# A routed layer on 28 tiles of 128 tokens in place of 32 batches of 112

## What is computed

```python
def _L3_ffn_ref(tokens, router_w, router_b, expert_weights):      # tokens 32 x 112 x 256
    logits = jnp.einsum('bsh,eh->bse', tokens, router_w) + router_b        # 8 experts
    probs = jax.nn.softmax(logits, axis=-1)
    top_p, top_i = jax.lax.top_k(probs, 2)
    w = top_p / (jnp.sum(top_p, axis=-1, keepdims=True) + EPS)
    y_all = jnp.einsum('nh,ehd->ned', x, expert_weights)                  # every token, every expert
    out = jnp.einsum('nk,nkh->nh', wf, y_k)                               # the two chosen, weighted
    ...
x = x + jnp.tanh(g_xattn[3]) * _L3_xattn_ref(_layernorm(x), ctx_1024, ctx_1024, mask, gamma, beta)
x = x + jnp.tanh(g_ffn[3]) * _L3_ffn_ref(_layernorm(x), router_w, router_b, expert_weights)
```

## Time and profile before

| | |
|---|---|
| median of 3 runs | 3184.21 us (3181.15 to 3189.6) |
| the profiled execution | 3165.71 us |
| its span, first to last instruction | 3163.5 us |
| PE busy | 3026.6 us, 96% |
| DVE busy | 2022.8 us, 64% |
| `masked_attention`, in the span | about 2789 to 2910 us |
| `routed_layer`, in the span | 2911 to 3163.5 us |

### The profile page before, as it was taken

One profiled execution on the slowest core, in us unless ns is written; L12 is line 12 of the kernel. 1 busy time (PEld: TensorE's weight loads), 2 busy tenths in 40 slices (PEclk: granted clock), 3 DMA queues, 4 the chain that ended last, 5 costly groups with the idle time before them and its releaser, 6 DMA issues. The chain is left out here.

```text
span 3163.5 us, 61263 instructions
## 1 busy us (share of the span) xinstructions
PE 3026.6 (96%) x23544; PEld 2306.6 (73%) x23544; DVE 2022.8 (64%) x4390; ACT 1456.5 (46%) x2845; POOL 626.3 (20%) x903
## 2 busy tenths in 40 slices
PE   8988999989899999999999999799999999899999
PEld 7875655667799999999999998566666666566443
DVE  4664111157577887778788876566666666588654
ACT  3431111135455555555555555466666666455000
POOL 3575000053000230122022000211112111045000
PEclk8998999999899999999999999899999999899999
DMA  9643233177200000000000000100000000255000
GB/s 275 185 145 115 80 120 120 54 212 247 83 2 1 2 2 1 2 1 2 1 2 2 1 1 2 36 16 21 20 18 21 16 21 11 76 171 168 15 15 18
DMA packets 75073, 181.80 MB, mean 57 GB/s; under 512 B 12102, under 2 KB 18739, under 8 KB 74453
## 3 DMA queue, kind: packets, MB, share of 16 engines
q1 hardware_dynamic: 58260, 137.83, 13.7%
q10 hardware_dynamic: 10192, 25.30, 2.6%
q0 software_dynamic: 6336, 14.76, 1.6%
HBM read 150.25 MB, written 27.79 MB: 56 GB/s over the span
## 5 line engine op out<-in xcount | busy, mean ns | idle before, releaser
L2786 ACT ACTIVATE probs<-probs,neg_top 112x375 f32<-112x375 f32 x512 | 281.8, 599 | 16.2 <-DVE neg_top L2709 15.0
L2709 DVE CUSTOM_DVE_ANT_0 probs<-ps,add 112x375 f32<-112x375 f32 x512 | 250.2, 546 | 58.8 <-PE ps L2860 55.1
L2266 DVE TENSOR_REDUCE top<-ps 112x16 f32<-112x1792 f32 x96 | 194.3, 2024 | 58.4 <-PE ps L2504 56.8
L3324 PE MATMUL ps<-we,xn_t 128*112 128x512 f32 x512 | 230.0, 613 | 0.9 <-PEq L813 0.9
L1646 DVE TENSOR_TENSOR hidden<-gated,ps 128x512 f32<-128x512 f32 x64 | 44.0, 688 | 284.6 <-PE ps L1689 284.6
L2716 DVE COPY probs_t<-ps 125x336 f32<-125x336 f32 x256 | 128.8, 503 | 151.4 <-PE ps L2887 151.4
L2887 PE MATMUL ps<-ident,probs 112*125 112x112 f32 x1536 | 222.5, 281 | 2.8 <-DVE probs_t L2716 2.8
L2887 PEld LDWEIGHTS ps<-ident,probs 112*125 112x125 f32 x1536 | 189.7, 188 | 30.7 <-issue 20.2
L2282 DVE TENSOR_TENSOR probs<-probs,inv_sum 112x1792 f32<-112x1792 f32 x96 | 197.2, 2054 | 3.3
L2278 DVE TENSOR_REDUCE row_sum<-probs 112x16 f32<-112x1792 f32 x96 | 193.9, 2020 | 4.3 <-ACT probs L2390 4.3
L2270 DVE TENSOR_TENSOR probs<-ps,top 112x1792 f32<-112x1792 f32 x96 | 194.3, 2024 | 3.3
(11 more groups left out here) (453 smaller groups left out, 6368.1 us busy)
## 6 DMA issues: line engine op xcount, KB each, us to landing
ctx_t<-in_ctx_T_dram SPq DMA_DIRECT2D x96, 375.0 KB, 4.4
ctx_sb<-in_ctx_dram ACTq DMA_DIRECT2D x64, 384.0 KB, 4.7
ctx_sb<-in_ctx_dram SPq DMA_DIRECT2D x32, 384.0 KB, 4.7
ctx_sb<-in_ctx_T_dram SPq DMA_DIRECT2D x32, 375.0 KB, 3.0
queue<-zeros SPq DMA_DIRECT2D x32, 256.0 KB, 5.2
rows<-queue SPq DMA_DIRECT2D x16, 512.0 KB, 4.8
outputs<-out SPq DMA_DIRECT2D x16, 512.0 KB, 2.9
mask_in<-in_mask_BxSxS_fk_dram SPq DMA_DIRECT2D x16, 328.1 KB, 5.8
```

The lines of the kernel that those rows point to most:

```text
L2266: dve.tensor_reduce(top[:, :, :], scores, AX.X, ALU.max).then_inc(s["top_done"], 1)
L2709: dve.tensor_tensor_reduce(out=probs[:, u, h, :], in0=k.ps[0:S, SCORE + h, 0:L], in1=add[:, j % 2, :], scale=1.0, scalar=BIG, op0=ALU.add, ...
L2786: act.activation(probs[:, u, h, :], probs[:, u, h, :], ACT.Exp, bias=neg_top[:, u, h:h + 1], scale=-1.0).then_inc(s["probs_done"], 1)
L3324: mm = pe.matmul(k.ps[0:S, Y + at % YB, :], xn_t[:, j + u, c, :], r.we[:, c, e:e + TWO, :].rearrange("p e d -> p (e d)"), start=c == 0, st ...
```

## The change

The routed layer takes the tokens in 28 tiles of 128 in place of 32 batches of 112.

- `x_sb` stays as it is for norms and transposes. A second tensor `x_tiles[128, 28, 256]` takes the same values as tiles. SP copies batch j into it after `residual_done` of that batch, by transfers from SBUF to SBUF (`load_routed_tiles`): a batch falls into one or two tiles, so each group of 8 batches takes 14 transfers of 112, 16+96, 32+80, 48+64, 64+48, 80+32, 96+16 and 112 rows of 1 KB, 56 in all. In SP's list those of batch j - 9 stand at the end of step j, those of the last nine batches behind the loop.
- The transposed tokens `xn_t` are stored as one row of 3584 tokens per chunk, so that a slice of 128 can straddle two batches. Transposes and copies out of PSUM stay at 112 tokens, 32 of each.
- `experts` runs over 14 pairs of tiles with 128 stationary columns; `routed_logits` runs 28 times instead of 32, each waiting for the batches under its tile; the add writes `x_tiles` and once a tile waits for `tiles_loaded` of its group of 7 tiles. `route_batches` and the other steps between the pairs stand behind the same pair numbers as before.
- The groups of `route_group` are 6, 8 and 14 tiles (before 8, 8 and 16 batches), and the logits of each tile have a place of their own in the PSUM bank.
- The output is stored from `x_tiles`, two tiles at a time, 14 stores.

```diff
@@ -67,7 +67,7 @@
-            sp.wait_ge(k.stored, 16 * (B // 2))
+            sp.wait_ge(k.stored, 16 * (TILES_R // 2))
...
-ROUTES = (0, NB, BODY, B)
+TILES_R = B * S // P
+TILES_G = NB * S // P
+ROUTES = (0, 6, 2 * TILES_G, TILES_R)
...
 def routed_copy(k, r, act, j):
 
     act.wait_ge(r.transposed, j + 1)
-    act.activation(r.xn_t[:, j, :, :], k.ps[:, R_XT + j % 2, 0:DC * S].rearrange("p (a t) -> p a t", a=DC), ACT.Copy).then_inc(r.xt_copied, 1)
-
-
-def routed_logits(k, r, pe, j, at):
-
-    pe.wait_ge(r.xt_copied, j + 1)
-    if j == 0:
+    act.activation(r.xn_t[:, :, j * S:(j + 1) * S], k.ps[:, R_XT + j % 2, 0:DC * S].rearrange("p (a t) -> p a t", a=DC), ACT.Copy).then_inc(r.xt_copied, 1)
+
+
+def routed_logits(k, r, pe, t):
+
+    pe.wait_ge(r.xt_copied, ((t + 1) * P + S - 1) // S)
+    if t == 0:
         pe.wait_ge(r.router_loaded, 32)
     for c in range(DC):
-        mm = pe.matmul(k.ps[0:S, R_LOGITS, at:at + E3], r.xn_t[:, j, c, :], r.rw_t[:, c, :], start=c == 0, stop=c == DC - 1)
+        mm = pe.matmul(k.ps[:, R_LOGITS, t * E3:(t + 1) * E3], r.xn_t[:, c, t * P:(t + 1) * P], r.rw_t[:, c, :], start=c == 0, stop=c == DC - 1)
     mm.then_inc(r.logits_done, 1)
+
+
+def routed_pieces(j):
+
+    first = j * S
+    out = []
+    while first < (j + 1) * S:
+        t, p = divmod(first, P)
+        count = min(P - p, (j + 1) * S - first)
+        out.append((first - j * S, count, t, p))
+        first += count
+    return out
...
+def load_routed_tiles(k, r, sp, j):
+
+    for s0, count, t, p in routed_pieces(j):
+        sp.dma_start(r.x_tiles[p:p + count, t, :], k.x_sb[s0:s0 + count, j, :]).then_inc(r.tiles_loaded[j // NB], 16)
...
-    r.rb = sb(nc, "rb", [S, E3], F32)
-    r.iota = sb(nc, "iota", [S, E3], F32)
-    r.iota_i = sb(nc, "iota_i", [S, E3], I32)
+    r.rb = sb(nc, "rb", [P, E3], F32)
+    r.iota = sb(nc, "iota", [P, E3], F32)
+    r.iota_i = sb(nc, "iota_i", [P, E3], I32)
+    r.x_tiles = sb(nc, "x_tiles", [P, TILES_R, D], F32)
+    r.tiles_loaded = [sem(nc, f"tiles{h}_loaded") for h in range(B // NB)]
...
-    r.xn_t = sb(nc, "xn_t", [P, B, DC, S], F32)
+    r.xn_t = sb(nc, "xn_t", [P, DC, B * S], F32)
...
+    TILE_LAG = 9
...
+                    if j >= TILE_LAG:
+                        sp.wait_ge(s["residual_done"], j - TILE_LAG + 1)
+                        load_routed_tiles(k, r, sp, j - TILE_LAG)
+                for j in range(B - TILE_LAG, B):
+                    sp.wait_ge(s["residual_done"], j + 1)
+                    load_routed_tiles(k, r, sp, j)
...
-                act.dma_start(r.rb[:, :], row(k.inputs["L3_ffn_router_b"]).partition_broadcast(S)).then_inc(r.router_loaded, 16)
+                act.dma_start(r.rb[:, :], row(k.inputs["L3_ffn_router_b"]).partition_broadcast(P)).then_inc(r.router_loaded, 16)
...
                 for j in range(2, NB, 2):
                     routed_transpose(k, r, pe, j)
                     routed_transpose(k, r, pe, j + 1)
-                    for i in (j - 2, j - 1):
-                        routed_logits(k, r, pe, i, i * E3)
-                for i in (NB - 2, NB - 1):
-                    routed_logits(k, r, pe, i, i * E3)
+                    for t in range(max(j - 3, 0), j - 1):
+                        routed_logits(k, r, pe, t)
+                for t in range(TILES_G - 2, TILES_G):
+                    routed_logits(k, r, pe, t)
...
-        logits = sb(nc, "logits", [S, B, E3], F32)
...
+        logits = sb(nc, "logits", [P, TILES_R, E3], F32)
...
-                for j in range(0, B, 2):
+                tiles = k.out.rearrange("b s d -> (b s) d").rearrange("(t p) d -> p t d", p=P)
+                for j in range(0, TILES_R, 2):
                     sp.wait_ge(s["added"], E3 * (j + 2))
-                    sp.dma_start(k.out[j:j + 2].rearrange("b s d -> s b d"), k.x_sb[:, j:j + 2, :]).then_inc(k.stored, 16)
+                    sp.dma_start(tiles[:, j:j + 2, :], r.x_tiles[:, j:j + 2, :]).then_inc(k.stored, 16)
...
-                    link(dve.tensor_tensor(logits[:, cut, :], k.ps[0:S, LOGITS, 0:n * E3].rearrange("p (g e) -> p g e", g=n),
-                                           r.rb[:, :].unsqueeze(1).broadcast_to([S, n, E3]), ALU.add))
+                    link(dve.tensor_tensor(logits[:, cut, :], k.ps[:, LOGITS, ROUTES[g] * E3:ROUTES[g + 1] * E3].rearrange("p (g e) -> p g e", g=n),
+                                           r.rb[:, :].unsqueeze(1).broadcast_to([P, n, E3]), ALU.add))
...
-                                x = batch(k.x_sb, j + u)
+                                x = r.x_tiles[:, j + u, :]
+                                if e == 0 and t == 0:
+                                    dve.wait_ge(r.tiles_loaded[(j + u) // TILES_G], 16 * sum(len(routed_pieces(b)) for b in range(NB)))
                                 if t == 0:
                                     dve.wait_ge(s["experts_done"], (j // 2 * (E3 // TWO) + e // TWO) * 2 + u + 1)
                                 if n >= 2:
                                     dve.wait_ge(s["added"], n - 1)
                                 at = (j // 2 * (E3 // TWO) + e // TWO) * 2 + u
-                                dve.scalar_tensor_tensor(x, k.ps[0:S, Y + at % YB, t * D:(t + 1) * D], weight[:, j + u, e + t:e + t + 1], x,
+                                dve.scalar_tensor_tensor(x, k.ps[:, Y + at % YB, t * D:(t + 1) * D], weight[:, j + u, e + t:e + t + 1], x,
                                                          ALU.mult, ALU.add).then_inc(s["added"], 1)
...
-                    for j in range(max(ROUTES[g], NB), ROUTES[g + 1]):
+                    for j in range(*((0, 0), (NB, BODY), (BODY, B))[g]):
                         routed_copy(k, r, act, j)
...
-                def route(j):
-                    g = group_of[j]
-                    pe.wait_ge(s["exps_ready"], g)
-                    routed_logits(k, r, pe, j, (j - ROUTES[g]) * E3)
+                def route(t):
+                    pe.wait_ge(s["exps_ready"], group_of[t])
+                    routed_logits(k, r, pe, t)
 
                 def experts(j):
                     for e in range(0, E3, TWO):
@@ -3321,19 +3352,19 @@
                                 pair, w = divmod(before, E3)
                                 pe.wait_ge(s["added"], pair * E3 * 2 + (w // 2 * TWO + TWO - 1) * 2 + w % 2 + 1)
                             for c in range(DC):
-                                mm = pe.matmul(k.ps[0:S, Y + at % YB, :], xn_t[:, j + u, c, :], r.we[:, c, e:e + TWO, :].rearrange("p e d -> p (e d)"),
+                                mm = pe.matmul(k.ps[:, Y + at % YB, :], xn_t[:, c, (j + u) * P:(j + u + 1) * P], r.we[:, c, e:e + TWO, :].rearrange("p e d -> p (e d)"),
                                                start=c == 0, stop=c == DC - 1)
                             mm.then_inc(s["experts_done"], 1)
 
                 def route_batches(h):
-                    for j in range(NB * h, NB * (h + 1)):
-                        routed_transpose(k, r, pe, j)
-                        if j > NB * h:
-                            route(j - 1)
-                    route(NB * (h + 1) - 1)
+                    for i in range(NB):
+                        routed_transpose(k, r, pe, NB * h + i)
+                        if i >= 2:
+                            route(TILES_G * h + i - 2)
+                    route(TILES_G * (h + 1) - 1)
...
-                for j in range(0, B, 2):
+                for j in range(0, TILES_R, 2):
                     experts(j)
                     if j == 4:
```

More of the change, by code:

```diff
@@ L3138, in routed_layer @@
         xn, xn_t = r.xn, r.xn_t
-        logits = sb(nc, "logits", [S, B, E3], F32)
-        top = sb(nc, "top", [S, B], F32)
-        exps = sb(nc, "exps", [S, B, E3], F32)
-        total = sb(nc, "total", [S, B], F32)
-        probs = sb(nc, "probs", [S, B, E3], F32)
-        best = sb(nc, "best", [S, B, 8], F32)
-        best_at = sb(nc, "best_at", [S, B, 8], U32)
-        best_f = sb(nc, "best_f", [S, B, 8], F32)
-        route1 = sb(nc, "route1", [S, B, E3], F32)
-        weight = sb(nc, "weight", [S, B, E3], F32)
-        weight_sum = sb(nc, "weight_sum", [S, B], F32)
-        gain = sb(nc, "gain", [S, B], F32)
+        logits = sb(nc, "logits", [P, TILES_R, E3], F32)
+        top = sb(nc, "top", [P, TILES_R], F32)
+        exps = sb(nc, "exps", [P, TILES_R, E3], F32)
+        total = sb(nc, "total", [P, TILES_R], F32)
+        probs = sb(nc, "probs", [P, TILES_R, E3], F32)
+        best = sb(nc, "best", [P, TILES_R, 8], F32)
+        best_at = sb(nc, "best_at", [P, TILES_R, 8], U32)
+        best_f = sb(nc, "best_f", [P, TILES_R, 8], F32)
+        route1 = sb(nc, "route1", [P, TILES_R, E3], F32)
+        weight = sb(nc, "weight", [P, TILES_R, E3], F32)
+        weight_sum = sb(nc, "weight_sum", [P, TILES_R], F32)
+        gain = sb(nc, "gain", [P, TILES_R], F32)
         LOGITS, Y, YB = R_LOGITS, 3, 5
@@ L3182, in each @@
                 def each(col):
```

(6 more changed lines are left out.)

## The result

| | before | after |
|---|---|---|
| median of six runs each | 3187.48 us | 3169.35 us |
| ratio, 95% interval | | 0.9938 [0.9924, 0.9951] |
| the profiled execution | 3165.71 us | 3169.83 us |
| first product of the third layer, from the span's start | 837.8 us | 860.8 us |
| first scores of the attention to first expert product | 119.6 us | 127.8 us |

The kernel is faster by 0.6%, 18.1 us, where 28.8 were forecast. On the forecast's own base the ratio gives 0.9938 x 3184.21 = 3164.5 us, 9 us above the forecast and inside its range; the median as measured is 3169.35, just above the range's upper end of 3169, as before stood 3.3 us higher beside it.

What follows compares the result with a forecast made beforehand. PE alone was taken to bound the routed layer. Expert products 27.5 plus router 1.6 less last store 0.3 gave 28.8 us off a median of 3184.2, so 3155.4 us; range 3147 to 3169.

Steps and rivals of the forecast that it cites:

- the forecast's own base: Median of the kernel before, 3184.2 us, from which the prediction subtracted its 28.8 us.
- Part 1: Routed layer's expert products: 64 records fewer at an unchanged 0.429 us each, a gain of 27.5 us.
- Rival 1: Columns cost: expert product records grow to 0.49 us, leaving only the router's gain, about 3183 us; chance 0.03.
- Part 2: Routed layer's router products: three fewer at 0.52 us, a gain of 1.6 us, bounds 0.5 to 2.
- Part 3: DVE in the routed layer: 224 adds for 256, hidden; route_group chains and the tiles_loaded wait cost 0.
- Part 4: TensorE's lower clock at the routed layer's start and behind each route_batches: loss stays 10.3 us, 3.5 either way.
- Part 6: The kernel's end: a last store of 256 KB instead of 224 KB, at most 0.3 us more.
- Part 5: Copies in SP's list during the attention before the routed layer: cost 0 to 4.5 us, taken as 0.
- the allowances for the clock and for the spread of the runs: In the forecast's range: clock 3.5 us either way, spread of the runs 3.1 us down and 5.4 up.
- The slack: In the attention, ctx_t lands in 5.4 us, ahead of need, so 6.8 us of DMA backlog hurt nobody.
- Rival 2: Crowded DMA: small copy pieces cost 1.6 us a batch, 15.6 us on the attention, 3171 us; chance 0.07.
- Rival 3: Copies hold SP's queue, each transfer delaying loads 2.3 us in the attention: 3240 us, slower; chance 0.03.

Runs made afterwards that it cites:

- e2: The kernel before plus x_tiles, its 56 copies and DVE's wait, with nobody reading the tiles: 3196.82 us, ratio 1.003.
- e7: The copies alone on the kernel before (e2), each batch in one transfer of 112 rows, 32 instead of 56: 3179.44 us in one run.
- e10: The copies alone on the kernel before (e2), only those of the odd batches, half the bytes: 3172.18 us in one run.
- e11: The copies alone on the kernel before (e2), as 16 transfers of two batches in 2 KB packets: 3176.75 us in one run.
- e5: The change with only 112 of each tile's 128 tokens in the expert products and adds: 3175.94 us in one run.
- e12: The change itself once more, side by side with late copies on the same chip: 3151.4 us, ratio 0.9956.
- e13: Late copies (e3) once more, side by side with the change on the same chip: 3143.66 us, ratio 0.993.
- e9: Late copies (e3) with the last route_group of 14 tiles cut into 6 and 8: 3140.12 us, ratio 0.9925.
- e4: The change with the eight expert weight loads (2 MB) moved behind the attention's loop, copies kept in it: 3161.71 us, ratio 0.9909.
- e8: The change with the loop's copies issued from ACT's queue instead of SP's, the last nine batches staying on SP: 3132.67 us in one run.
- e6: The change with x_tiles filled from the input x in HBM by the same 56 transfers: 3144.73 us in one run.
- e3: The change with the copies late: 16 batches behind the attention's loop, the others at the head of the routed layer's SP list: 3163.76 us, ratio 0.9915.

## Why the forecast was 10 us off, step by step

**Part 1, the products: right.** 64 records by 0.429; the layer went from 252.4 to 224.9 and 224.0, -27.5 and -28.4, and four more profiles with before's own layer (e2, e7, e10, e11) read 252.2 to 253.6. The weight load grew from 0.18 to 0.20 us on the mean and stayed covered. Rival 1 is out by e5.

**Part 2, the router: right in sign, too large.** 1.6 us were forecast. The three `route_batches` take 5.66, 6.07 and 5.51 us after (from the end of one stretch of products to the start of the next), 17.2 in all, and 17.9 in e12 and 17.8 in e13, where the earlier trace rows has 17.95: a gain of 0 to 0.7. Two things failed. The step in the earlier trace rows is the longer of two kinds: in the same phase of before they alternate,

```profile
2955.71 0.31 PE ps L719 x4
2956.02 0.24 PE ps L703 x2
2956.26 0.52 PE ps L719 x4
```

so a product is 0.42 on the mean and not 0.52. With 128 columns its steps are 0.43 to 0.45 long, but for the last, so seven take 3.1 us where eight took 3.3; and the first product, which waits for a second copy, starts 1.1 us into the phase and not 0.7. I had put that in a bound and priced it at nothing.

**Part 3, DVE: the condition I named came up, at no net cost.** I had written that, if the clock didn't fall behind the last `route_batches`, DVE's chain would make PE wait. In the profile of after it fell only in part:

```profile
3063.70:3075.00 11.30, 10.86 (x24) 0.85 0.01 2
```

0.85, where before has 0.74 over the first 11.3 us behind its last `route_batches`, and after 20 records PE's weight load waits for the adds behind the group of 14:

```profile
3075.10 0.30 PEld L3355 LDWEIGHTS ps<-we,xn_t 128*128 128x128 f32 x2 [1.37 <-DVE x_tiles L3289]
```

From the first of these 224 records to the end of the last are 3162.93 - 3064.03 = 98.90 us. In e12 the clock was at 0.75 over the same 11.3 us, nobody waited, and the 224 records took 99.07. What the clock doesn't take, DVE's chain does. That is also why cutting the group in e9 gave nothing: there the clock was at 0.75 as well, and no wait was left to remove. It would pay only in an execution where the clock stays up, which is argued and not shown. The 16 adds, and `tiles_loaded`, cost nothing, as forecast.

**Part 4, the clock: right.** 202.7 us of records against 448 x 0.429 = 192.2: 10.5 lost, 10.3 forecast. Part 6: the store lands in 2.1 us; nothing.

**Part 5, the copies: here it failed.** Taken at 0, measured 8.2 us in the profile of after and 4.2 in e12, with a bound of 4.5 that was too low. That the time still lies in the range is luck in part: the allowances for the clock and for the spread of the runs, which weren't needed, covered what this bound lacked. Four steps of it:

1. *Which batches count.* I priced the 14 batches of the stretch, since it has the weights and the highest share. e4 shows that the queue builds before it. The loop copies 23.
2. *What one costs.* The bounds, 0.38 to 0.80 us of all engines a batch, were right; the end that I leaned on wasn't. Over the attention the two queues take 83.7% of 127.8 us after and 72.8% of 119.6 us before, 19.9 us more of all engines for 32 batches, 0.62 each on the mean. Late, with nothing beside them, 16 batches cost (77.3% of 119.8) - 87.1 = 5.5 us, 0.34 each, near the stores that I had taken as the nearest row. The same copy costs the engines nearly twice as much in the crowd, where it slows its neighbours too. A price for a busy place has to be read in a busy place.
3. *The slack.* 6.8 us was about right, and is a sum for the whole loop: in the change the load of batch 23 landed after 11.8 us in time, that of batch 24 after 14.3 us late, and 5.4 + 6.8 is 12.2. With these two sizes the prediction's own formula gives 23 x 0.62 - 6.8 = 7.5 us; if the nine batches behind the loop cost 0.34, the 23 cost 0.73 and it gives 10.0. Measured were 4.2 to 11.1.
4. *The room.* I held 339 GB/s of wanted rate against the 368 of the earlier trace rows. That row is another mix in another stage. This loop got 288 to 298 GB/s in all nine profiles with a backlog, and its own demand without the weights is (375 + 384 + 164) KB in 3.42 us, 276 GB/s; the copies bring it to 310. So the copies alone lift it over what it gets then, and the landing times drift upwards, a fifth of a microsecond for each microsecond, until PE is reached. But 288 to 298 isn't a fixed limit. Before, the weights (256 KB every second step) bring the demand to 314, of which 307 were moved, and the landing stays at 5.4; in e10 half the copies come on top of that, 305 are moved, and it lands in 6.5. Where the edge lies between half the copies and all, and why the rate is lower behind it, the runs don't show.

Of the waits in this part the claim held that SP's order does no harm (the issue times in the section on the result, and e8's landings), though the size was off: two pieces take SP 1.2 us to issue and not 0.66,

```profile
2871.10 0.34 SPq L808 DMA_DIRECT2D ctx_t<-in_ctx_T_dram  x1
2871.49 1.16 SPq L740 DMA_DIRECT2D x_tiles<-x_sb  x2
```

0.58 for each transfer from SBUF to SBUF, 0.33 for a load. **Rival 2**, which had this place for 0.07, was right that the engines are crowded, and wrong in why: it isn't because the pieces are small (e7, e11). Its clue was in the same paragraph, the share of 0.99, and I set against it that the landings were at 5.4 us. That only tells that the queue doesn't grow yet; it says nothing on how near the edge is. **Rival 3** is out by e7 and e8.

**What the sum leaves.** Forecast -28.8; Part 5's miss +8.2, Part 2's +0.9 to 1.6, the rest under 1: about -19, the stages' -19.3 and the medians' -18.1. For e12 and e13 the stages give -24.2 and -27.7; the medians give -15.7 and -23.5, the ratios -14 (the interval reaches from -9 to -18) and -22. The first product of the third layer stands at 843.9 and 844.9 there, and how much of the difference is that early part can't be said, as before has no profile on that chip. This remains open.

## What to carry to other kernels

A DMA share near 1 with steady landing times is an edge, not a reserve: compare the rate wanted with what the same mix of transfers is given when it is full, which takes a run to learn, and count every step in which the new transfers run, not just the densest. If a transfer has a wide due time, put it behind the loads of the loop and not beside them; here that was worth all of the 4 to 11 us, for a few lines. Moving them to a computing engine's queue isn't the same: there each copy held that engine's own next instruction back by up to 0.6 us (e8). And where one row of a pattern carries a price, look at its neighbour first; steps alternate.

## What the runs showed of the hardware

- **With a backlog the DMA engines move less than without.** With landings of `ctx_t` at a median of 9.5 us and more, 288 to 298 GB/s at a share of 1.04 to 1.06 (9 profiles, 51 us each). The same loop with late copies moves 305 GB/s at a share of 0.98 (e13), and with half the copies 305 at 1.04 (e10), both with peaks near 400 and landings of 5.5 and 6.5 us; so the share alone doesn't tell the two apart. The mean packet is 1.9 to 2.2 KB in all. The time of all engines for a MB is 0.99 x 51 / 15.67 = 3.2 us before and 1.06 x 51 / 15.16 = 3.6 after. Whether this is the memory, SBUF's side or the switching among more transfers in flight was not told apart; e6 and e11 say that it's neither the copies' source nor their packets alone. The Trainium skill ("DMA: Bandwidth & Descriptors", Bandwidth) gives each of two cores that stream together roughly 358 GB/s of device memory. One core runs here, its first layer moved 368, and this loop stays well below either, so no run here shows that limit.
- **Issuing a transfer costs the issuing engine time.** SP takes 0.33 us for a load of 375 KB and 0.58 for a copy from SBUF to SBUF; on ACT's queue a copy takes 0.6 us, and ACT's next instruction starts behind it (e8).
- **The early part of the program differs by up to 34 us from one execution to another,** whichever the kernel: the third layer's first product stands between 834.6 and 868.4 us in 14 profiles. From there to the first scores of the attention 11 of them take 1953.2 to 1954.5 us, e2 and e4 3 us less and e8 9 less, in code that is the same in all. The attention of before's kind (before, e3, e9, e10, e13) is 119.6 to 119.9 us and the layer repeats within 1.4. A stage's effect below 1% is to be read from its own start, not from spans.
